# Grouped attention: in two of four steps the pick of a raw head's squares stands behind the next raw head's products

## What is computed

```python
ln_out = _ln(hidden_states, ln_w, ln_b)
q = _fp8_linear_pertensor(ln_out, wq, wq_scale, q_in_scale).reshape(b, s, g, hpg, d)
q = _ln(q, qln_w, qln_b)
k = _ln(_fp8_linear_pertensor(ln_out, wk, wk_scale, k_in_scale).reshape(b, s, g, d), kln_w, kln_b)
v = _fp8_linear_pertensor(ln_out, wv, wv_scale, v_in_scale).reshape(b, s, g, d)
core = _gqa(q, k, v).reshape(b, s, nh * d)
qx = _fp8_linear_pertensor(ln_out, wqx, wqx_scale, qx_in_scale).reshape(b, s, g, hpg, d)
qx = _ln(qx, qxln_w, qxln_b)
kx, vx = jnp.split(jnp.einsum('bsi,oi->bso', cond, w_kv_x), 2, axis=-1)
kx = _ln(kx.reshape(b, sc, g, d), kxln_w, kxln_b)
xout = _gqa(qx, kx, vx.reshape(b, sc, g, d)).reshape(b, s, nh * d)
catq = _div_clamp_fp8(jnp.concatenate([core, xout], axis=-1), proj_smooth)
return jnp.einsum('bsi,oi->bso', catq, wproj) * (proj_in_scale * proj_w_scale)
```

## Time and profile before

| | |
|---|---|
| median of 3 runs | 2041.06 us (2039.13 to 2041.79) |
| profiled execution | 2039.61 us, span of the core 2037.8 us |
| grouped attention in it | about 207 to 1077 us |
| TensorE busy | 1979.5 us, 97% of the span |
| VectorE / ScalarE / GpSimd busy | 1414.6 / 1225.3 / 688.3 us |

### The profile page before, as it was taken

One profiled execution on the slowest core, in us unless ns is written; L12 is line 12 of the kernel. 1 busy time (PEld: TensorE's weight loads), 2 busy tenths in 40 slices (PEclk: granted clock), 3 DMA queues, 4 the chain that ended last, 5 costly groups with the idle time before them and its releaser, 6 DMA issues. The chain is left out here.

```text
span 2037.8 us, 31350 instructions
## 1 busy us (share of the span) xinstructions
PE 1979.5 (97%) x11032; PEld 1560.7 (77%) x11032; DVE 1414.6 (69%) x3154; ACT 1225.3 (60%) x3186; POOL 688.3 (34%) x689
## 2 busy tenths in 40 slices
PE   8999999999999999999998999999999999999998
PEld 5644789889888988898986895666656786666997
DVE  2397677777777676767667847676777658996555
ACT  2073688878887878888774444544534446772332
POOL 1300344544545454545431001333252102332442
PEclk9999999999999999999998999999999999999999
DMA  4033434243424242342332203323131330003200
GB/s 188 10 120 127 137 87 151 73 149 87 152 71 151 87 132 90 108 130 70 110 101 83 99 1 132 125 104 129 61 151 75 115 102 22 2 2 147 86 1 33
DMA packets 60173, 193.66 MB, mean 95 GB/s; under 512 B 9408, under 2 KB 28640, under 8 KB 56048
## 3 DMA queue, kind: packets, MB, share of 16 engines
q1 hardware_dynamic: 48496, 172.15, 25.0%
q10 hardware_dynamic: 9504, 8.50, 1.4%
q0 software_dynamic: 2016, 11.01, 1.3%
HBM read 171.75 MB, written 19.48 MB: 94 GB/s over the span
## 5 line engine op out<-in xcount | busy, mean ns | idle before, releaser
L988 PE MATMUL psum<-la_w_both,context 128*128 128x256 f32 (+1 forms) x1536 | 343.6, 380 | 0.0
L988 PEld LDWEIGHTS psum<-la_w_both,context 128*128 128x128 f32 (+1 forms) x1536 | 277.4, 184 | 44.8
L1465 POOL TENSOR_TENSOR norm_std<-room 128x400 f32<-128x400 f32 x75 | 70.2, 937 | 271.6 <-DVE room L1230 271.5
L944 PE MATMUL psum<-qa_xqf,qa_two 128*128 128x400 f32 x640 | 156.2, 372 | 2.4 <-PEq L60 2.4
L944 PEld LDWEIGHTS psum<-qa_xqf,qa_two 128*128 128x128 f32 x640 | 115.4, 191 | 7.5 <-issue 3.2
L3029 ACT ACTIVATE itp_w_q<-psum,it_nm 100x257 f32<-100x257 f32 (+1 forms) x256 | 101.5, 414 | 26.3 <-DVE it_nm L3058 25.5
L1458 POOL TENSOR_TENSOR room<-room,qa_inv 128x500 f32<-128x500 f32 x64 | 89.6, 1400 | 53.2 <-DMA qa_inv<-qa_std_rows 51.0
L1006 PE MATMUL psum<-qa_kxT,room 128*100 128x361 f32 x256 | 100.5, 474 | 4.2 <-ACT qa_kxT L1148 3.1
L1154 ACT ACTIVATE qa_prob<-psum,qa_nm 100x361 f32<-100x361 f32 x128 | 71.8, 561 | 47.9 <-DVE qa_nm L1319 47.4
L1154 ACT ACT_TABLE_LOAD x64 | 82.1, 1283 | 24.0 <-ACT qa_size L1172 18.2
L2568 POOL TENSOR_TENSOR gf_last_diff<-la_gf_what,la_gf_w 128x512 bf16<-128x512 bf16 x24 | 27.0, 1146 | 200.6 <-issue 164.4
(11 more groups left out here) (396 smaller groups left out, 5309.3 us busy)
## 6 DMA issues: line engine op xcount, KB each, us to landing
context<-in_context SPq DMA_DIRECT2D x70, 722.0 KB, 4.6
qa_inv<-qa_std_rows SPq DMA_DIRECT2D x64, 250.0 KB
qa_w_raw<-in_qa_w SPq DMA_DIRECT2D x8, 1536.0 KB, 15.4
la_gf_raw<-in_gf_w SPq DMA_DIRECT2D x16, 768.0 KB, 4.7
qa_piece<-in_tf_pieces ACTq DMA_DIRECT2D x64, 128.0 KB, 2.1
la_w_qt<-in_qa_o SPq DMA_DIRECT2D x8, 1024.0 KB, 7.1
gf_ternary<-la_gf_made POOLq DMA_DIRECT2D x7, 768.0 KB
gf_ternary<-keep POOLq DMA_DIRECT2D x7, 768.0 KB
```

The lines of the kernel that those rows point to most:

```text
L944: mm = pe.matmul(psum[:, bank, 0:HALF], two[:, part, j, k, :], xqf[:, PART_XQ[j], k, (h % 2) * HALF:(h % 2 + 1) * HALF], start=(k == 0 and ...
L988: mm = pe.matmul(psum[0:rows, i // 2, (i % 2) * 256:(i % 2) * 256 + 256], ctxT[:, n % 2, k, t0:t0 + rows], kv_raw[:, s, k, :], start=(k == ...
```

## The change

In steps n > 2 with n % 4 of 0 or 1 in which a unit stands in `behind(n)`, the picks of the step before (one unit, two matmuls) are issued behind the second half of that unit and ahead of the output projection, and no longer behind the values. These are the steps 4, 5, 8, 9, ... 56, 57. In all others the order stays. The other engines' programs stay as they are, and the waits are those inside `variance`.

```diff
             def step(g, s, b, n):
                 project_values(g, s, b, n)
-                for u in units_of(n - 1) if n > 1 else FIRST[-2:] if n == 0 else ():
-                    variance(u)
+                beside_raw = n > 2 and n % 4 < 2 and behind(n)
+                if not beside_raw:
+                    for u in units_of(n - 1) if n > 1 else FIRST[-2:] if n == 0 else ():
+                        variance(u)
                 for u in ahead(n):
                     project_unit(u)
                 if n == 1:
@@ -1062,6 +1064,8 @@
                     turn_probs(n - 1)
                 for u in behind(n) if around else ():
                     project_unit(u, range(C // 2, C))
+                for u in units_of(n - 1) if beside_raw else ():
+                    variance(u)
                 if not early(n, OUT_LAG):
                     project_out(*out_chunk(g, b, n))
                 if not early(n, 1):
```

## The result

| | before | changed |
|---|---|---|
| median, 14 runs each | 2040.68 us (2038.82 to 2042.18) | 2044.57 us (2042.57 to 2047.26) |
| profiled execution, span | 2039.61, 2037.8 us | 2045.22, 2043.4 us |
| steps 4 to 59 in its trace | 764.29 us | 769.57 us |
| a regular step, phase 0 / 1 | 13.17 to 13.19 / 13.19 to 13.20 us | 13.45 / 13.43 to 13.45 us |
| steps 14, 22, ... 54 | 14.87 to 14.89 us | 14.64 to 14.65 us |

The change makes the kernel slower: ratio 1.0020, 95% interval 1.0014 to 1.0027, which is 2.9 to 5.5 us on 2040.7. The forecast was 2047.0 us in a range of 2044 to 2051, +5.9 us; the medians say +3.9 and the steps of the trace +5.3.

What follows compares the result with a forecast made beforehand. TensorE's own queue bounds the kernel, the picks covering a wait for the keys. Per step 0.37 - 0.14 + 0.05 = +0.28 us; 26 x 0.28 = 7.3, minus 1.4, gives +5.9 us on 2041.06: 2047.0 us, range 2044 to 2051.

Steps and rivals of the forecast that it cites:

- The wait under the picks: Behind the values, scores wait for the turned keys' copy: removing the picks gains 0.14 us a step, not 0.45, minus 0.05.
- the sum of 4.6: Alternative total in us if TensorE pulls weight loads across the scores' wait: 26 x 0.23 - 1.4.
- The 0.05: Scores' first pair takes 0.66 us instead of 0.61, with no matmul ahead to hide its weight load: 0.05 us more.
- Rival A: Scores gain nothing and stay at 1.09 us behind the values: +9.5 us, 2050.6 us; chance 0.15.
- The pair's new price: The two picks between raw head and output projection are paid in full: 0.37 us a step, upper bound 0.45.
- Steps 4 and 5 free: Before any output projection, the moved picks fall into TensorE's idle time behind the raw head's second half: cost 0.
- The late squares: In steps 14, 22, ... 54 the unmoved pick's wait for GpSimd's low squares goes: 6 x 0.24 = -1.4 us.
- Rival B: Late squares stay late, their chain following the scores or the turning, not the step's start: +7.3, 2048.4 us; chance 0.14.
- C: Scores wait for TensorE's queue only: 0.45 won, 0.37 paid in 28 steps; -3.6 us, 2037.4 us; chance 0.05.
- D: No effect, a reordering of a full queue: removed 0.45 and added 0.45, 2041 us; chance 0.06.

Runs made afterwards that it cites:

- e3: Kernel before with two slots for the turned keys, scores taking the previous step's keys, so no wait for fresh ones: median 2037.51 us, ratio 0.9985.
- e4: Changed kernel with two slots for the turned keys, scores taking the previous step's keys, so no wait for fresh ones: median 2037.41 us, ratio 0.9985.
- e5: Kernel before with only the picks of steps n % 4 = 0 (4, 8, ... 56) moved: median 2042.91 us, ratio 1.0014.
- e6: Kernel before with only the picks of steps n % 4 = 1 (5, 9, ... 57) moved: median 2041.04 us, ratio 1.0005.
- e10: Changed kernel with the pick of steps n % 4 = 2 also moved behind the unit ahead: median 2044.43 us, ratio 1.0020.
- e12: Kernel before with one GpSimd instruction (L1483, low output weights) moved behind the scaling of the next step's heads: median 2039.56 us against 2039.54.
- e1: Changed kernel with the 56 pick matmuls of n % 4 = 0 and 1 left out from step 4 on: median 2037.76 us, ratio 0.9988 against before.
- e2: Changed kernel plus two useless 400-column matmuls behind the values in the 28 steps, where the picks stood: median 2046.76 us, ratio 1.0033 against before.
- e7: Kernel before with the pick of steps n % 4 = 2 moved behind the eight matmuls of the unit ahead: median 2037.72 us, ratio 0.9986.
- e11: Repeat on another chip of the kernel before with the n % 4 = 2 pick moved behind the unit ahead: median 2038.06 us, ratio 0.9989.
- e8: The changed kernel itself, run again beside the versions that move the picks of n % 4 = 0 or 1 alone: median 2044.46 us, ratio 1.0021.
- e9: Kernel before, unchanged, run as if it were a changed one: median 2039.58 us against 2039.95, ratio 0.9998.

## Why the prediction was right, and where it was off

*The wait under the picks.* Right: scores at 0.95 (said: 0.95 to 0.96), first pair 0.66, 26 bare waits, and e3 and e4 show that it is the keys' wait. The first pair's weight load starts at 593.42 in step 28, behind the wait and 0.03 us ahead of its matmul, so the sum of 4.6, with weights loaded across the wait, doesn't hold. The 0.05 has its size right and its reason in part: 0.03 of it stands in e4 without any wait. Both prices had been read from steps 60 to 63, before any pick was moved, and from the end of the copy, not from the time at which those steps start their scores. Rival A took that time, 1.10, and would have given +9.5; the trace after refutes it, and shows why: in steps 60 to 63 ScalarE is late with the heads, and in the moved steps it isn't.

*The pair's new price.* 0.36 us for 0.37. With it a regular step was to be 13.46 us and is 13.45 in phase 0. In phase 1 it is 13.43 to 13.45, for two small differences that I hadn't seen: in n % 8 = 5 L1027 started 0.37 us behind L1025 before and starts 0.34 us behind it now, and in n % 8 = 1 L1025 started 1.47 us behind L1041 and starts 1.45 behind it now. So the term 26 x 0.28 = 7.3 was 13 x 0.27 + 13 x 0.25 = 6.7 us.

*Steps 4 and 5 free.* Right: 12.96 and 13.19 us. TensorE's idle time behind the raw head takes the pair in.

*The late squares.* Right: -0.24 us six times, 1.4 us. It was close: the step ahead is longer by 0.25, and 0.24 was needed. e5 and e6 show that it is the longer step ahead that does it, e10 that nothing else is left, and e12 what makes them late, a cause that the prediction didn't have (it named VectorE's chain as a whole). Rival B falls with them.

*Rivals C and D.* Both need an early copy. e1 and e2 measure a pair in the old place at 0.1 us, not 0.45; e3 and e4 make the copy early, and then the change is worth next to nothing. C's gain of 0.08 us a step doesn't come even so: in e4 against e3 the regular steps of phases 0 and 1 together are 0.65 us longer, since the next waits begin there, and the late squares give the same back. C's sum was also wrong in itself: it kept the 1.4 us of the late squares, which come from a longer step, and under C the step would be shorter.

*The sum.* Forecast 7.3 - 1.4 = 5.9; in the steps 6.7 - 1.4 = 5.3, twice to 0.1 us. The forecast of the median, 2047.0, is 2.4 above the 2044.57 measured: 0.6 is this sum, 0.4 that the median of three runs of before (2041.06) lay above that of fourteen (2040.68), and 1.4 is the gap below. The lower edge doesn't come out of the prediction's own terms either: a pair at 0.36 gives 26 x 0.27 - 1.4 = 5.6, so 2046.7, and 1.4 lower is 2045.3, not 2044.5. The measured median lies below that and only 0.6 above the edge of 2044. The mechanism was right; that the median fell into the range is in part luck.

*What stays open:* the medians say 3.9 and 4.0, the steps 5.3. That is a ratio of 1.0026, inside the intervals, and traces of one kernel differ by more than 1 us ahead of step 4 (262.5 and 260.3 us for the changed kernel; 258.7 to 262.5 over all fourteen traces) and behind the steps (1012.6 and 1011.4 us from step 60 on for e7 and e11). But all eight kernels of e1 to e8 lie 1.0 to 1.5 us lower against before than their steps up to 63 say. They were measured on two chips, each with runs of before of its own (medians 2040.48 of 27 and 2040.46 of 33), so that one odd median of before doesn't explain it. The control (e9) has 0.4 us, with an interval of 1.8 us to either side, and beside it e10 is at +4.9 over e9 and e11 at -1.5, which the steps (+4.9, -1.8) give; in e12 the difference has the other sign (the median 0.0, the steps -0.6). The cause isn't known.

## What to carry to other kernels

Work between a producer and its waiting consumer in an in-order queue can be cover that no idle row betrays: before moving it, put the end of what the consumer waits for beside the start of the consumer without that work, and look for a stretch of the same loop where the work is missing. Here a pair was worth 0.45 us by its rows and 0.09 to 0.10 by its removal (e2, e1). Move the work that waits itself, not the work that covers a wait.

## What the runs showed of the hardware

VectorE's `tensor_scalar` on 128 x 400 int16 (L1352) takes 0.26 us alone and 1.21 to 1.24 us when a GpSimd `tensor_tensor` is running as it begins, and then it ends 0.12 us behind GpSimd's; in before that holds in 32 of 64 steps. e12 shows it as the cause: with GpSimd's operation moved away, 63 of 64 take 0.26 to 0.27 us. A VectorE `tensor_tensor` with two inputs (L1272) ends 0.55 us behind the GpSimd operation that was running as it began, 0.43 or 0.67 us into it. The Trainium skill (GPSIMD Engine Reference, Specifications, SBUF interfaces) says that GpSimd's are shared with VectorE, with contention for VectorE's 2-port modes or for two SBUF inputs. The trace agrees for the two-input L1272. L1352 has one input; whether it runs in such a mode no trace here shows.

The first matmul of 400 columns behind matmuls of 128 columns costs about 0.08 us more than one behind its like, whether it is the pick (0.45 against 0.36 for the pair, before and after) or the unit (1.53 against 1.46 for the eight, e7 and before).
